# Gated cross-attention and mixture of experts: setup merged into the attention program, later loads placed behind the first placements, gelu parts in another order

## The chip, the cores and the metric

The kernel runs on one core of a Trainium2 chip. The metric is the device time of one execution in microseconds (us). Three runs of the kernel before took 1938.36, 1944.8 and 1937.91 us; the median is 1938.36. A core has TensorE (matmul, called PE in the profile, with PEld for its weight loads), VectorE (DVE), ScalarE (ACT), GpSimd (POOL) and SyncE (SP), which issues most transfers here.

## The reference

x is 16 x 512 x 512, the context 16 x 512 x 1024. First comes a gated cross-attention with 16 heads of 32, then a gated mixture of 8 experts of which each token takes two:

```
q = layernorm(x);  k, v = split(ctx_2048)
logits = (q * 32**-0.5) @ k.T + b + (-1e12) * (position >= seq_len)
x = x + tanh(g_xattn) * softmax(logits) @ v

y = layernorm(x)
route = normalise(y) @ normalise(centroids).T + y @ w_route.T
gates = softmax over the two largest of route
h = gelu(y @ w1[e] + b1[e])
x = x + tanh(g_ffn) * sum over e of gates[e] * (h @ w2[e] + b2[e])
```

Everything is float32.

## The kernel before

The program has four blocks of engine programs, one behind another. Each ends on all engines before the next begins.

The **setup** block (L305 to L400) loads the sequence lengths, b, the gates, the centroids and w_route with seven small transfers on SP. VectorE fills rows 96 to 127 of the two stacks stA and stB with ones (L344, L345), then makes the bias and mask rows for all batches (L348 to L368, stored to HBM at L316), the normalised centroids (L358, L362, the inverse square root of 13 steps at L371, L373), and constant tiles for the later tables (L375 to L381). GpSimd makes iotas, the identity and triangle tiles (L321 to L340), ScalarE two tanh values (L388, L389), TensorE the turned routing weights (L397, L398), which VectorE copies (L383).

The **attention** block is a software pipeline over 64 groups (16 batches, 4 groups of 4 heads each). Every engine runs the same list of steps, numbered from -8 (FIRST) to 70, fully unrolled, and every engine's order inside a step is written out by hand in 16 sub-steps. In step l the logits, exp and value products are those of group l; the max product (stB against stA, L823) with its row maxima (L998) is that of group l + 2; the placing of turned queries and keys in the stacks is that of group l + 3. So the first placement is in step -3, the first max product in step -2, the first logits (L811) in step 0. A placement is six SP transfers of 256 KB (L484), from SBUF to SBUF, after four small ones with the bias rows (L513). The negated maxima go to stB the same way in the step before the logits (L533).

Once a batch, x and the keys are loaded two batches ahead (L497, L498, steps with l divisible by 4), the values one batch ahead (L505), the residual at L554. VectorE takes the statistics of x (L982, L989), GpSimd makes the query scale out of them (`query_scale`, L607 to L623, called at L648) and regroups the keys (L604), ScalarE normalises x into the queries (L687), and TensorE turns queries and keys (L798); ScalarE takes the high part (L698), VectorE the low part (L974). Batch 0's and batch 1's x and keys and batch 0's values are the first five transfers of the block.

A short piece of **table** steps (L1054 to L1100) sorts the tokens by expert.

The **block loop** (L1198 to L1448) then runs over blocks of 512 tokens of one expert, in steps that each do the front of one block and the back of the block before. It is a hardware loop of 18 rounds with two steps in its body. In a step TensorE turns the gathered rows (`turn`, L1283) in two pairs, with the second product of the block before between and behind them (`second`, first half L1318, second half L1322), then the token ranks (L1293) and the first product of this block, m = 0 and m = 1, each 12 matmuls (L1332). ScalarE and VectorE split each float32 operand in a high and a low part. After the first product ScalarE does gelu (L1373) for m = 0 and 1 and then the high parts (L1376) for both; VectorE does the low parts (L1437) for both at the end of its step, behind the search for the tokens of a later block (`find_tokens`, L1434). The second product's half m waits for low part m (f_hs, L1299). VectorE also makes the low part of the expert's first weights (L1416), a 128 x 1024 subtraction. GpSimd gathers the rows of the next block with four indirect transfers (L1233), waits for the output rows of ScalarE (L1260; L1365 makes them), and adds them to the output with four more (L1263). Two tiny instructions on GpSimd, `carry_wait` (L1229), tell the other engines how far it is.

## Time and profile before

| | |
|---|---|
| Median of three runs | 1938.36 us |
| The profiled execution | 1941.25 us |
| Its span | 1939.5 us, 32926 instructions |
| TensorE busy | 1733.0 us (89%) |
| VectorE busy | 1381.7 us (71%) |
| GpSimd busy | 1249.5 us (64%) |
| ScalarE busy | 1170.1 us (60%) |
| Mean granted TensorE clock | 0.98 |

In the page's picture of 40 slices (48.5 us each) TensorE is at 0, 5 and then 9 tenths up to slice 28; slices 29 to 31 hold the tables at 6 to 9 tenths with a granted clock that falls to 5 and 7 tenths in two slices, and from there to the end it is at 9 or 8 tenths again. VectorE is at 5 tenths in the first slice, GpSimd at 2, ScalarE at 1. The chain of work that ended last is read from its end back; here it consists of GpSimd's indirect transfers (L1233 7% of the span, L1263 5%) and of issue time.

In a timeline row the first number is the start, the second the time that the merged instructions of the row cover. In brackets stands how long the engine was idle before it and what ended that. TensorE works at one of two levels, 1.2 and 2.4 GHz; the column with the granted clock says which share of the higher it was given.

### The profile page before, as it was taken

The page shows a single profiled execution, that of the slowest core. Times are in us where ns is not written, and L with a number is a line of the kernel's source. Part 1 is how long each engine was busy: PE and PEld are TensorE (multiplying, and loading weights), DVE is VectorE, ACT ScalarE, POOL GpSimd, SP SyncE. Part 2 cuts the span into 40 slices and gives each one's busy share as a digit, 9 for nine tenths or more (in the row PEclk, how much of TensorE's full clock was granted, in tenths as well). Part 3 has the DMA queues.
Part 4 walks back from the last instruction along what each step waited for, and adds up shares of the span by engine and source line. Part 5 has one row for each costly group of instructions (what it writes and reads, how often), then busy time and mean ns, then how long its engine had stood idle before and what let it go on. Part 6 is the DMA issues. An engine that isn't in the chain of part 4 may idle for free. (4 is left out here: it accounts for less than half of the span.)

```text
span 1939.5 us, 32926 instructions
## 1 busy us (share of the span) xinstructions
PE 1733.0 (89%) x9696; PEld 1039.5 (54%) x9697; DVE 1381.7 (71%) x2983; ACT 1170.1 (60%) x2044; POOL 1249.5 (64%) x1507
## 2 busy tenths in 40 slices
PE   0599999999999999999999999984699989999897
PEld 0244555555555555555555555533477767777775
DVE  5568778878878778788778787733666666665665
ACT  1066677676776776776766767663355555555554
POOL 2057577585675776675766857550577777777776
PEclk9999999999999999999999999995799999999999
DMA  3888899898898998998998979643488787868774
GB/s 111 100 175 168 129 203 160 150 208 145 159 193 160 169 183 139 191 179 132 200 154 159 198 112 188 121 133 97 89 153 148 144 142 139 154 130 148 134 146 65
DMA packets 173069, 291.46 MB, mean 150 GB/s; under 512 B 37983, under 2 KB 42079, under 8 KB 172945
## 3 DMA queue, kind: packets, MB, share of 16 engines
q1 hardware_dynamic: 140016, 222.26, 59.2%
q0 software_dynamic: 32928, 67.68, 20.0%
q8 instruction: 61, 1.00, 0.3%
q14 instruction: 64, 0.52, 0.1%
HBM read 127.09 MB, written 71.63 MB: 102 GB/s over the span
## 5 line engine op out<-in xcount | busy, mean ns | idle before, releaser
L998 DVE TENSOR_REDUCE bank<-bank 128x1 f32<-128x512 f32 x1024 | 696.2, 690 | 256.4 <-PE bank L823 248.2
L714 ACT ACTIVATE prob<-bank 128x512 f32<-128x512 f32 x1024 | 593.0, 597 | 359.1 <-PE bank L811 357.7
L659 POOL TENSOR_TENSOR prob<-prob 128x512 f32<-128x512 f32 x256 | 320.7, 1289 | 325.9 <-PE bank L771 325.9
L811 PE MATMUL bank<-stB,stA 100*128 100x512 f32 x1024 | 477.1, 467 | 19.7 <-ACT prob L714 13.6
L823 PE MATMUL bank<-stA,stB 98*128 98x512 f32 x1024 | 423.6, 416 | 31.7 <-DMA stA<-regrouped_then_w 17.5
L811 PEld LDWEIGHTS bank<-stB,stA 100*128 100x128 f32 x1024 | 193.4, 189 | 253.3 <-ACT prob L714 177.5
L663 POOL TENSOR_TENSOR prob<-prob 128x512 f32<-128x512 f32 x256 | 320.3, 1290 | 0.0
L771 PE MATMUL bank<-prob,vin 128*32 128x512 f32 x2048 | 272.7, 605 | 0.7 <-ACT prob L714 0.7
L1263 POOL DMA_INDIRECT out_dram<-yout,scatter_ids x144 | 226.4, 1572 | 52.6 <-issue 52.0
L1195 PE MATMUL bankb<-w_hi,gelu_parts 128*128 x576 | 199.1, 406 | 47.2 <-DVE gelu_parts L1437 47.2
L823 PEld LDWEIGHTS bank<-stA,stB 98*128 98x128 f32 x1024 | 197.9, 193 | 79.2 <-DVE bank L998 37.1
L1233 POOL DMA_INDIRECT rows_in<-xn_rows,gather_ids x152 | 183.6, 1208 | 85.9 <-DVE rows_in L1444 44.9
L1195 PE MATMUL bankb<-turned_parts,w_parts 128*128 128x512 f32 x888 | 218.2, 401 | 0.0
L1195 PEld LDWEIGHTS bankb<-turned_parts,w_parts 128*128 128x128 f32 x888 | 165.4, 190 | 37.6
L1195 PEld LDWEIGHTS bankb<-w_hi,gelu_parts 128*128 128x128 f32 x576 | 108.2, 188 | 78.7 <-issue 55.5
L1347 ACT ACTIVATE turned_parts<-bankb 128x512 fp32r<-128x512 f32 x148 | 82.7, 596 | 94.8 <-PE bankb L1283 83.4
L1365 ACT ACTIVATE yout<-out_with_bias,row_gates 128x512 f32<-128x512 f32 x144 | 92.4, 712 | 61.3 <-DVE out_with_bias L1428 61.3
L1437 DVE TENSOR_TENSOR gelu_parts<-gelu,gelu_parts 128x512 fp32r<-128x512 f32 x74 | 47.8, 688 | 107.0 <-ACT gelu_parts L1376 107.0
L784 PE MATMUL bank<-prob,ones 128*32 128x512 f32 x1024 | 123.1, 598 | 0.0
L1373 ACT ACTIVATE gelu<-bankb,b1s 128x512 f32<-128x512 f32 x74 | 51.0, 689 | 113.8 <-PE bankb L1195 113.8
L1195 PE MATMUL bankb<-regrouped_then_w,gelu_parts 128*128 x288 | 114.2, 397 | 0.0
L687 ACT ACTIVATE regrouped_then_w<-x_k_then_w,q_shift,rstd 128x512 f32<-128x512 f32 x64 | 83.1, 1307 | 37.3 <-POOL q_shift L623 37.3
(181 smaller groups left out, 2234.1 us busy)
## 6 DMA issues: line engine op xcount, KB each, us to landing
stB<-regrouped_then_w SPq DMA_DIRECT2D x192, 256.0 KB, 5.9
stA<-regrouped_then_w SPq DMA_DIRECT2D x192, 256.0 KB, 6.8
x_k_then_w<-in_x_dram SPq DMA_DIRECT2D x16, 1024.0 KB, 8.2
x_k_then_w<-in_ctx_dram SPq DMA_DIRECT2D x16, 1024.0 KB, 12.5
vin<-in_ctx_dram SPq DMA_DIRECT2D x16, 1024.0 KB, 9.3
xres<-in_x_dram SPq DMA_DIRECT2D x16, 1024.0 KB, 6.9
out_dram<-xres SPq DMA_DIRECT2D x16, 1024.0 KB, 7.5
xn_rows<-xn SPq DMA_DIRECT2D x64, 256.0 KB, 5.4
```

What stands on the lines that cost most here:

```text
L659: pool.tensor_tensor(first[:, j, :], first[:, j, :], more[:, j, :], ALU.add).then_inc(s_acc, 1)
L663: pool.tensor_tensor(first[:, j, :], first[:, j, :], then[:, j, :], ALU.add).then_inc(s_acc, 1)
L714: act.activation(prob_of(st, 0, u)[:, j, :], psS[j % 2][:, :], ACT.Exp).then_inc(s_exp, 1)
L771: last = pe.matmul(psO[DH * j:DH * (j + 1), :], vin[:, vpar, kt, c0:c0 + DH], p[:, j, :], start=(u == 0), stop=(u == NT - 1), skip_group_c ...
L784: last = pe.matmul(bank[DH * j:DH * (j + 1), :], ones[:, 0:DH], p[:, j, :], start=(u == 0), stop=(u > 0), skip_group_check=True, tile_posi ...
L811: pe.matmul(psS[j % 2][:, :], stA[0:100, g, j, kt * P:(kt + 1) * P], stB[0:100, g, j, :], start=True, stop=True).then_inc(s_qk, 1)
L823: pe.matmul(psM[s % 2][:, :], stB[0:98, g, j, i * P:(i + 1) * P], stA[0:98, g, j, :], start=True, stop=True).then_inc(s_m, 1)
L998: dve.tensor_reduce(mx[:, s // 4, s % 4:s % 4 + 1], psM[s % 2][:, :], AX.X, ALU.max).then_inc(s_mx, 1)
L1195: last = pe.matmul(bank, wts(p), mov(q), start=start and i == 0, stop=stop and i == 2)
L1233: pool.indirect_dma_start(rows[:, par, c, :], None, xn_d, bass.IndirectOffsetOnAxis(ap=gids[:, par, c:c + 1], axis=0), bounds_check=TOK - ...
L1263: pool.indirect_dma_start(out_rows, bass.IndirectOffsetOnAxis(ap=sids[:, h, c:c + 1], axis=0), yout[:, h, c, :], None, bounds_check=TOK - ...
L1365: act.activation(yout[:, st.h, c, :], ysum[:, c, :], ACT.Copy, scale=gate[:, st.h, c:c + 1]).then_inc(f_yo, 1)
```

## The change

It has three parts.

1. The setup's work is no longer a block of its own but stands inside the attention block. SP issues three of the small loads, then batch 0's x and keys, then the other four small loads, waits for the bias rows, stores them, and waits for both fills. The fill of stA goes from VectorE to ScalarE (four copies of a constant), that of stB to GpSimd, behind its constant tiles. VectorE does the bias steps first (`set_bias`, step -8), then the statistics of batch 0, then the query scale of batch 0 (`query_scale` takes the engine as an argument; later batches stay on GpSimd), then the centroid steps and constant tiles (`set_routes`). TensorE turns the routing weights in step -2 into another bank.
2. Batch 1's x is loaded behind the placement of step -3, batch 0's values behind that of step -2, batch 1's keys behind the maxima of step -1. VectorE's statistics of batch 1 come ten sub-steps later in steps -2 and -1.
3. In the block loop ScalarE does gelu 0, high part 0, gelu 1, high part 1. VectorE does low part 0 at the end of its step and low part 1 in the next step, behind the first two turned parts.

The diff, cut to its core (the moved instructions are otherwise the same):

```diff
+                SET_POOL = 14
+                SET_BIAS = 12
+                SET_DVE = 17 + RSQRT_STEPS
...
-                with nc.Block() as block:
-                    @block.sync
-                    def _(sp):
-                        sp.dma_start(len_i[:, :], lens.rearrange("b a -> a b").to_broadcast([P, B])).then_inc(s_load, 16)
...
-                        sp.dma_start(wro, w_route).then_inc(s_load, 16)
-                        sp.wait_ge(s_dve, 13)
-                        sp.dma_start(bm_d, b_split[:, :, :].bitcast(F32)).then_inc(s_put, 16)
-                        sp.wait_ge(s_put, 16)
-                    @block.gpsimd
...
-                    def _(pool):
-                        pool.iota(pos_i, pattern=[[1, BLK]], base=0, channel_multiplier=0).then_inc(s_pool, 1)
-                        pool.iota(pos4_i[:, :], pattern=[[P, BLK // P]], base=0, channel_multiplier=1).then_inc(s_pool, 1)
...
-                    def _(dve):
-                        dve.memset(stA[96:P, :, :, :].bitcast(F32), 1.0)
-                        dve.memset(stB[96:P, :, :, :].bitcast(F32), 1.0)
-                        dve.wait_ge(s_load, 16 * 7)
-                        dve.wait_ge(s_pool, 3)
-                        dve.tensor_copy(pos4[:, :], pos4_i[:, :]).then_inc(s_dve, 1)
-                        dve.tensor_copy(len_f[:, :], len_i[:, :]).then_inc(s_dve, 1)
...
-                    def _(act):
-                        act.wait_ge(s_load, 16 * 7)
...
@@ -461,6 +368,24 @@
                 for n in range(FIRST, G + LAST):
                     step(Step(None, n, G))
+            def query_scale(eng, st):
+                b = (st.l + 4) // 4
+                par = b % 2
+                c = lambda k: b * LN1 + k
+                eng.wait_ge(s_stat, 8 * (b + 1))
...
+                def load_batch(b):
+                    par = b % 2
+                    sp.dma_start(xin[:, par, :, :], x_d[b:b + 1].rearrange("a p i d -> p (a i) d")).then_inc(s_x[par], 16)
+                    sp.dma_start(kin[:, par, :, :], c_d[b:b + 1, :, :, 0:D].rearrange("a p i d -> p (a i) d")).then_inc(s_k[par], 16)
+                def load_v(b):
+                    sp.dma_start(vin[:, b % 2, :, :], c_d[b:b + 1, :, :, D:2 * D].rearrange("a p i d -> p (a i) d")).then_inc(s_v[b % 2], 16)
...
                     if st.g() == 0:
-                        par = (st.l // 4) % 2
-                        if st.on(8):
-                            if st.rnd is not None or st.l >= 0:
...
-                            sp.dma_start(kin[:, par, :, :], c_d[bass.ds(b, 1), :, :, 0:D].rearrange("a p i d -> p (a i) d")).then_inc(s_k[par], 16)
-                    if st.g() == 1 and st.on(4):
-                        par = (st.l // 4 + 1) % 2
-                        if st.rnd is not None or st.l >= 4:
+                        if st.on(8) and st.l >= 0:
+                            sp.wait_ge(s_xg, st.batch(1, 0, 1))
+                            sp.wait_ge(s_kg, st.batch(1, 0, 1))
+                            load_batch(st.batch(1, 8, 0))
+                        if st.l == FIRST:
+                            sp.dma_start(len_i[:, :], lens.rearrange("b a -> a b").to_broadcast([P, B])).then_inc(s_load, 16)
+                            sp.dma_start(len_c[:, 0:1], lens).then_inc(s_load, 16)
+                            sp.dma_start(b_row, b_in.rearrange("(a s) -> a s", a=1).to_broadcast([B, S])).then_inc(s_load, 16)
+                            load_batch(0)
+                            sp.dma_start(gates_in[:, 0:1], g_xattn.rearrange("(a s) -> a s", a=1).to_broadcast([P, 1])).then_inc(s_set, 16)
+                            sp.dma_start(gates_in[:, 1:2], g_ffn.rearrange("(a s) -> a s", a=1).to_broadcast([P, 1])).then_inc(s_set, 16)
+                            sp.dma_start(cen, cent).then_inc(s_set, 16)
+                            sp.dma_start(wro, w_route).then_inc(s_set, 16)
+                            sp.wait_ge(s_dve, SET_BIAS)
+                            sp.dma_start(bm_d, b_split[:, :, :].bitcast(F32)).then_inc(s_put, 16)
+                            sp.wait_ge(s_put, 16)
+                            sp.wait_ge(s_ones, 2)
+                    if st.g() == 1 and st.on(4) and st.l >= 0:
+                        if st.l >= 4:
                             sp.wait_ge(s_pv, st.batch(4 * PV, 0, 0))
-                        b = st.batch(1, 4, 0)
-                        sp.dma_start(vin[:, par, :, :], c_d[bass.ds(b, 1), :, :, D:2 * D].rearrange("a p i d -> p (a i) d")).then_inc(s_v[par], 16)
+                        load_v(st.batch(1, 4, 0))
                     if st.on(3):
                         g = st.g(3)
...
                         i, before = turn_of(st, "TK")
                         sp.wait_ge(s_took[i], before + 1)
                         place_rows(stA, 1, g, 1, turnedL)
+                    if st.l == -3:
+                        sp.dma_start(xin[:, 1, :, :], x_d[1:2].rearrange("a p i d -> p (a i) d")).then_inc(s_x[1], 16)
+                    if st.l == -2:
+                        load_v(0)
                     if st.on(1):
                         i, before = turn_of(st, "MT")
...
                         for t in range(2):
                             sp.dma_start(stB[98 + t:99 + t, st.g(1), :, :].bitcast(F32), mT[HG * t:HG * t + HG, :].bitcast(F32)).then_inc(s_md[(st.l + 1) % 2], 16)
+                    if st.l == -1:
+                        sp.dma_start(kin[:, 1, :, :], c_d[1:2, :, :, 0:D].rearrange("a p i d -> p (a i) d")).then_inc(s_k[1], 16)
                     if st.g() == 1 and st.on(-5):
...
                         if st.rnd is not None or st.l >= 8:
                             sp.wait_ge(s_x1[par], st.bpair(16, 0, 0))
                             sp.wait_ge(s_xn2, st.count(1, -4, 0))
+                        if st.l == 0:
+                            sp.wait_ge(s_dve, SET_DVE)
...
+                pool.wait_ge(s_pool, SET_POOL)
+                pool.memset(stB[96:P, :, :, :].bitcast(F32), 1.0).then_inc(s_ones, 1)
+                pool.wait_ge(s_ones, 2)
                 def step(st):
+                    if st.l == -4:
+                        pool.wait_ge(s_ln1, LN1)
+                    elif st.g() == 0 and st.on(4):
+                        query_scale(pool, st)
                     if st.g() == 0 and st.on(4):
-                        query_scale(st)
                         regroup_k(st)
...
+                act.wait_ge(s_pool, 8)
+                for g in range(NG):
+                    last = act.activation(stA[96:P, g, :, :].rearrange("p h s -> p (h s)"),
+                                          ones[96:P, 0:1].to_broadcast([P - 96, HG * S]), ACT.Copy)
+                last.then_inc(s_ones, 1)
+                act.wait_ge(s_set, 16 * 4)
+                act.activation(tanh_a[:, :], gates_in[:, 0:1], ACT.Tanh).then_inc(s_act, 1)
+                act.activation(tanh_f[:, :], gates_in[:, 1:2], ACT.Tanh).then_inc(s_act, 1)
+                act.wait_ge(s_act, 2)
                 all_steps(act, step)
...
+                def turn_routes():
+                    pe.wait_ge(s_set, 16 * 4)
+                    pe.wait_ge(s_dve, SET_DVE - 2)
+                    for k in range(KD):
+                        pe.transpose(psO[:, 2 * E * k:2 * E * k + E], cen2[:, k * P:(k + 1) * P], ident[0:E, 0:E])
+                        last = pe.transpose(psO[:, 2 * E * k + E:2 * E * k + 2 * E], wro[:, k * P:(k + 1) * P],
+                                            ident[0:E, 0:E])
+                    last.then_inc(s_pe, 1)
                 def step(st):
+                    if st.l == -2:
+                        turn_routes()
                     for s in range(16):
                         u, j = s // 4, s % 4
...
                             kt, g = NT - 1 - u, st.g()
+                            if st.l == 0 and s == 0:
...
                             last.then_inc(done, 1)
...
+                def set_bias():
+                    dve.wait_ge(s_load, 16 * 3)
+                    dve.wait_ge(s_pool, 3)
+                    dve.tensor_copy(len_cf[:, 0:1], len_c[:, 0:1]).then_inc(s_dve, 1)
+                    dve.tensor_copy(pos[:, :], pos_i).then_inc(s_dve, 1)
+                    dve.tensor_copy(len_f[:, :], len_i[:, :]).then_inc(s_dve, 1)
...
+                    dve.wait_ge(s_dve, 9)
+                    dve.tensor_tensor(b_split[:, 1, :], b_all, b_split[:, 0, :].bitcast(F32),
+                                      ALU.subtract).then_inc(s_dve, 1)
+                    dve.tensor_copy(pos4[:, :], pos4_i[:, :]).then_inc(s_dve, 1)
+                    dve.tensor_copy(qcol[:, :], qcol_i[:, :]).then_inc(s_dve, 1)
...
+                def set_routes():
+                    dve.wait_ge(s_set, 16 * 4)
+                    dve.tensor_tensor_reduce(cen2, cen, cen, 1.0, 0.0, ALU.mult, ALU.add,
+                                             cn[:, 0:1]).then_inc(s_dve, 1)
+                    dve.wait_ge(s_dve, SET_BIAS + 1)
+                    dve.tensor_scalar(cn[:, 1:2], cn[:, 0:1], NORM_EPS * NORM_EPS, None, ALU.max).then_inc(s_dve, 1)
...
+                    rsqrt(dve, cn[:, 0:1], cn[:, 2:3], cn[:, 1:2], s_dve, lambda k: SET_BIAS + 2 + k)
+                    dve.wait_ge(s_dve, SET_BIAS + 2 + RSQRT_STEPS)
+                    dve.tensor_scalar(cen2, cen, cn[:, 0:1], None, ALU.mult).then_inc(s_dve, 1)
+                    dve.memset(ranks[0:TILES, :, :], float(P)).then_inc(s_dve, 1)
...
+                def take_routes():
+                    dve.wait_ge(s_pe, 1)
+                    dve.tensor_copy(routeT[:, :, :], psO[:, 0:KD * 2 * E].rearrange("p (k e) -> p k e", k=KD)).then_inc(s_dve, 1)
                 def step(st):
+                    if st.l == FIRST:
+                        set_bias()
+                    if st.l == -4:
+                        query_scale(dve, st)
+                        set_routes()
+                    if st.l == -2:
+                        take_routes()
                     for s in range(16):
...
                             route(st, s)
-                        if st.g() in (2, 3) and s in (0, 3) and st.on(8 - st.g()):
-                            stats(st, 2 * (st.g() - 2) + s // 3)
-                        if st.g() in (2, 3) and s in (2, 4) and st.on(8 - st.g()):
-                            aggregate(st, 2 * (st.g() - 2) + s // 4)
+                        late = 10 if st.l in (-2, -1) else 0
+                        if st.g() in (2, 3) and s - late in (0, 3) and st.on(8 - st.g()):
+                            stats(st, 2 * (st.g() - 2) + (s - late) // 3)
+                        if st.g() in (2, 3) and s - late in (2, 4) and st.on(8 - st.g()):
+                            aggregate(st, 2 * (st.g() - 2) + (s - late) // 4)
...
@@ -1371,7 +1412,6 @@
                                 act.wait_ge(f_hs, st.front(KE, -1, m + 1))
                             act.activation(gelu[:, m, :], psH[m][:, :], ACT.Gelu, bias=b1s[:, st.par(), m:m + 1]).then_inc(f_g, 1)
-                        for m in range(KE):
                             act.wait_ge(f_g, st.front(KE, 0, m + 1))
                             act.activation(hT[:, 0, m, :], gelu[:, m, :], ACT.Copy).then_inc(f_hhi, 1)
@@ -1385,6 +1425,11 @@
                     def take_turned(st, k):
                         dve.wait_ge(f_xhi, st.front(KD, 0, k + 1))
                         dve.tensor_tensor(xTb[:, 1, k, :], bank_of(st, USE[k])[:, :], xTb[:, 0, k, :].bitcast(F32), ALU.subtract).then_inc(f_use, 1)
+                    def gelu_lo(st, off, m):
+                        dve.wait_ge(f_hhi, st.front(KE, off, m + 1))
+                        dve.tensor_tensor(hT[:, 1, m, :], gelu[:, m, :], hT[:, 0, m, :].bitcast(F32), ALU.subtract).then_inc(f_hs, 1)
                     def mark_tiles(blk, expert):
@@ -1412,6 +1457,8 @@
                         mark_tiles(st.block(2), expert_ahead)
                         take_turned(st, 0)
                         take_turned(st, 1)
+                        if not st.first:
+                            gelu_lo(st, -1, 1)
                         dve.wait_ge(f_whi, st.front(1, 0, 1))
                         dve.tensor_tensor(w1p[:, 1, :, :], weights_of(w1_all, expert), w1p[:, 0, :, :].bitcast(F32), ALU.subtract).then_inc(f_wlo, 1)
                         take_turned(st, 2)
@@ -1432,9 +1479,7 @@
                         dve.tensor_copy(sids[:, st.par(), :], gids[:, st.par(), :]).then_inc(f_sid, 1)
                         dve.wait_ge(f_sid, st.steps(1, 0, 1))
                         find_tokens(bank_of(st, USE[KD]), st.block(2), st.par(), lambda per, k: st.steps(per, 2, k))
-                        for m in range(KE):
-                            dve.wait_ge(f_hhi, st.front(KE, 0, m + 1))
-                            dve.tensor_tensor(hT[:, 1, m, :], gelu[:, m, :], hT[:, 0, m, :].bitcast(F32), ALU.subtract).then_inc(f_hs, 1)
+                        gelu_lo(st, 0, 0)
```

## Rows read from the trace of the kernel before

**Rows 1.** Timeline from the start, setup: start us, us, engine, line, operation [idle before <- releaser].
```profile
5.51 0.20 ACT L388 ACTIVATE tanh_a<-xT 128x1 f32<-128x1 f32 x1 [3.45 <-DMA xres<-in_L_ffn_w_route_dram]
...
11.10 6.88 DVE L345 MEMSET stB<- 32x8192 f32 x1 [1.66 <-issue]
...
18.00 0.17 DVE L348 CAST positions_by_chunk<-xT 128x4 f32<-128x4 int32 x1
...
22.35 0.32 SPq L316 DMA_DIRECT2D bias_mask_rows<-xres  x1
...
22.43 0.14 DVE L121 TENSOR_SCALAR xT<-xT 8x1 int32<-8x1 int32 x1
...
24.77 0.47 DVE L373 TENSOR_SCALAR xres<-xres,xT 8x512 f32<-8x512 f32 x1
...
29.29 0.41 SPq L497 DMA_DIRECT2D x_k_then_w<-in_x_dram  x1
...
34.83 0.69 DVE L982 BATCH_NORM_STATS2 regrouped_then_w<-x_k_then_w 128x6 f32<-128x512 f32 x1 [5.82 <-DMA x_k_then_w<-in_x_dram]
```

**Rows 2.** Timeline of the attention program's start.
```profile
38.21 0.26 POOL L616 TENSOR_SCALAR varx<-mv 128x4 f32<-128x4 f32 x1 [34.55 <-DVE mv L989]
...
43.11 4.44 ACT L687 ACTIVATE regrouped_then_w<-x_k_then_w,q_shift,rstd 128x512 f32<-128x512 f32 x4 [37.30 <-POOL q_shift L623]
...
49.38 2.01 SPq L484 DMA_DIRECT2D stB<-regrouped_then_w  x3
...
64.22 0.77 PE L823 MATMUL bank<-stA,stB 98*128 98x512 f32 x1 [14.65 <-DMA stA<-regrouped_then_w]
...
98.41 0.79 PE L811 MATMUL bank<-stB,stA 100*128 100x512 f32 x1 [3.50 <-DMA stB<-regrouped_then_w]
```

**Rows 3.** Waits, 1385 to 1940 us: us in total, times, longest us.
```profile
POOL hold L1229 <- ACT yout L1365: 47.7, 34, 11.2
...
PE bankb L1195 <- DVE gelu_parts L1437: 47.2, 36, 1.4
```

**Rows 4.** Timeline of GpSimd alone in the block loop.
```profile
1704.69 1.55 POOL L1263 DMA_INDIRECT out_dram<-yout,scatter_ids  x1 [0.30 <-issue]
...
1717.58 1.54 POOL L1263 DMA_INDIRECT out_dram<-yout,scatter_ids  x1 [0.30 <-issue]
...
1722.85 1.98 POOL L1233 DMA_INDIRECT rows_in<-xn_rows,gather_ids  x1 [0.31 <-issue]
...
1725.13 1.00 POOL L1233 DMA_INDIRECT rows_in<-xn_rows,gather_ids  x1 [0.30 <-DMA out_dram<-yout,scatter_ids]
...
1734.92 1.54 POOL L1263 DMA_INDIRECT out_dram<-yout,scatter_ids  x1 [0.31 <-issue]
...
1749.70 1.55 POOL L1263 DMA_INDIRECT out_dram<-yout,scatter_ids  x1 [0.30 <-issue]
```
**Rows 5.** Timeline of one step of the block loop.
```profile
1714.07 0.69 ACT L1373 ACTIVATE gelu<-bankb,b1s 128x512 f32<-128x512 f32 x1 [1.10 <-PE bankb L1195]
...
1716.87 0.69 ACT L1373 ACTIVATE gelu<-bankb,b1s 128x512 f32<-128x512 f32 x1 [2.12 <-PE bankb L1195]
...
1717.46 1.14 ACT L1376 ACTIVATE gelu_parts<-gelu 128x512 fp32r<-128x512 f32 x2
...
1718.11 1.29 DVE L1437 TENSOR_TENSOR gelu_parts<-gelu,gelu_parts 128x512 fp32r<-128x512 f32 x2 [2.88 <-ACT gelu_parts L1376]
...
1719.04 0.50 PE L1195 MATMUL bankb<-w_hi,gelu_parts 128*128 x1 [1.33 <-DVE gelu_parts L1437]
...
1722.70 1.21 DVE L1416 TENSOR_TENSOR w_parts<-x_k_then_w,w_parts 128x1024 fp32r<-128x1024 f32 x1
```

**Rows 6.** Busy time by stretch; last three columns: granted clock, DMA share, GB/s.
```profile
30.00:40.00 10.00, 0.00 (x0) 0.00 (x0) 3.15 (x8) 0.00 (x0) 1.30 (x7) 1.00 0.93 329
...
90.00:100.00 10.00, 5.91 (x12) 3.02 (x12) 5.39 (x11) 0.60 (x1) 1.32 (x7) 1.00 1.07 180
```

137 lines of the change are left out of this document (50 added, 87 removed).

## The prediction

> **What bounds the kernel now.** I read the chain that ended last first. It lies wholly on GpSimd's indirect DMAs in the block loop and says nothing of the first 1300 us, so I then read the timeline from the start, and the waits and the timeline of single block steps. The span has three parts. Up to the first logit matmul at 98.41 us TensorE does almost nothing; from there to about 1300 us it is busy without a break; from about 1386 us the block loop runs 36 steps with a period of 15.1 us. The change touches the first part and the third. The middle starts earlier or later with the first part and keeps its length, because TensorE bounds it and nothing of it is edited.
>
> In the first part the reader is to see a sequence with hardly any overlap. Two VectorE fills of 6.88 us (the second begins at 11.10) stand ahead of every setup step, so the steps begin at 18.00 us and the first load is issued at 29.29, though all small loads were there by 5.51 [rows 1]. Then x arrives (34.83), VectorE takes the statistics, GpSimd makes the query scale (38.21 to 43.11), ScalarE normalises, and the first placement goes out at 49.38 [rows 1, 2]. From 49.38 the DMA engines set the pace: the max product starts only at 64.22 when the rows are placed, and the first logits, two placements later, at 98.41 [rows 2].
>
> In the block loop two bounds lie close together. TensorE waits 47.2 us in total, 36 times, for the low gelu part of VectorE; GpSimd waits 47.7 us, 34 times, for the output rows of ScalarE, 11.2 us of it once at the start, so 1.1 us in each of the others [rows 3]. Two steps take 1734.92 - 1704.69 = 30.23 us, 15.11 each [rows 4]. Without its wait TensorE would need 15.11 - 47.2/36 = 13.80; GpSimd without its wait 15.11 - 1.1 = 14.0. So the reorder can gain 1.3 us a step at most, and 1.1 if GpSimd stays as it is.
>
> **Part 1, the setup inside the attention program.** The x load goes from being SP's first DMA of a second block (29.29) to its fourth. Three small loads stand ahead of it; at 0.4 to 0.5 us for one issue (the x load takes 0.41 [rows 1]) it goes out near 2.2. Its landing took 34.83 - 29.29 = 5.54 us [rows 1], so x is there at 7.7. The bias steps on VectorE now come before the statistics: 22.35 - 18.00 = 4.35 us with the centroid reduction of about 0.7, which moves out, so 3.7 to 4.0 [rows 1]. They start when three small loads have landed, at about 4 and surely by 5.51 [rows 1], and end at 8.0 to 9.5. So the statistics start near 8.0 instead of 34.83: 26.8 us earlier. The first query scale moves from GpSimd (43.11 - 38.21 = 4.90 for 17 small steps [rows 2]) to VectorE, where 13 such steps on a narrower tile took 24.77 - 22.43 = 2.34, 0.18 each [rows 1]; 17 at 0.2 are 3.5, a further 1.4. ScalarE's normalising then starts 28.2 us earlier, at 14.9.
>
> What could be late instead: the two fills. The one of stA is now four ScalarE copies of 2048 elements. A 512-element copy takes 0.57 (1.14 for two [rows 5]), so at most 4 x 4 x 0.57 = 9.1 us from 2.4 on, 11.5. The tanh pair then waits for small loads that stand behind 2 MB, near 11, and ends by 13.5: hidden before 14.9, 1.4 us to spare. The fill of stB on GpSimd has no row of its own; VectorE takes 6.88 for the shape [rows 1], which gives 3.7 to 10.6, and twice that ends at 17.5. SP needs both only before the first bias rows, and those must be out by 21.2 (49.38 - 28.2). The centroid steps and rank fills (at most 29.29 - 22.35 = 6.9 us and the 0.7 of the reduction [rows 1]) come after the query scale, end near 22, and can hold the first low part back by 0.8, behind two placements that are queued anyway. I cost these at nothing; without that cover each is worth 1 to 3 us.
>
> **Part 2, the second batch's loads behind the placements.** Before, five loads of 1 MB moved at 329 GB/s while nothing else wanted the DMA engines [rows 6], 3.2 us each. Now x of batch 1, v of batch 0 and k of batch 1 are queued behind placements 0, 1 and 2. Between the landing of a placement and the issue of the next lie some 2.4 us, so the first two cost 3.2 - 2.4 = 0.8 each. The third meets DMA engines whose share is 1.07 from 90 to 100 us [rows 6], where batch 2's x and k follow, so I charge it in full, 3. Sum 4.6, bounds 0 and 9.6. SP is also held behind them only for their issue, 0.5 each. The late statistics of batch 1 (steps -2 and -1, moved by ten sub-steps of about 0.8) find x landed, and GpSimd's scale is wanted only at the key regroup of step 0.
>
> Part 1 and 2 give 28.2 - 4.6 = 23.6. Here a row speaks against the plan: gathers on GpSimd that take 1.00 us take 1.98 when VectorE runs its 1024-wide subtraction with both inputs in SBUF (1722.70 to 1723.91; the gather ends 0.9 us after it) [rows 4, 5]. The two engines do block one another. If the long GpSimd fill (3.7 to 10.6) holds VectorE's casts the same way, the bias steps start at 10.6 rather than 4 to 5.5 and x is no longer the last to come: 5 to 6 us lost. I cannot tell from before, where VectorE was inside a fill while GpSimd worked. The Trainium skill ("SBUF — State Buffer", Who interferes with whom) calls the shared port pair an exclusive lock that is held for a whole instruction, with casts and tensor_scalar among the operations that want it; by it VectorE would stand still until the fill ends. I take 23.6 for the start, since GpSimd is the one that is held in the rows shown, and keep 18 as rival (e); bounds 15 and 28.
>
> **Part 3, gelu order.** In the traced step the products of m=0 are done at 1714.07, of m=1 at 1716.87, and ScalarE then does gelu 1, copy 0, copy 1, so that VectorE starts low part 0 at 1718.11 and TensorE its second product at 1719.04 after 1.3 us of idling [rows 5]. Afterwards copy 0 follows gelu 0 at 1714.7; VectorE comes to low part 0 when the token search is done, near 1715.3, and ends it at 1716.0, before TensorE asks for it (its turns end near 1717.7). The wait is gone. Low part 1 goes into the next step behind two turned parts; it is ready some 1 us before TensorE reaches the second half. No table load shows between gelu and copy [rows 5], so alternating them costs nothing. Late next are TensorE itself (13.8) and GpSimd (14.0). GpSimd's 14.0 holds the stretching of gathers, 1.0 us in the step shown. The subtraction that causes it now starts about 1.6 us earlier against TensorE's own work, while GpSimd falls back to be the later one, so part of the overlap should slide off the gathers onto the scatters; and scatters beside a two-input subtraction show no stretch (1.54 at 1717.58, beside 1718.11) [rows 4, 5]. I take 13.9 a step: 1.2 x 36 = 43, rounded to 42 for the first and last steps. Bounds: 54 (also the turns' waits for VectorE gone, an estimated 13.6) and 12 (each step as in rival a).
>
> **Sum.** 23.6 + 42 = 65.6 us. The profiled run took 1941.25 with a span of 1939.5, so its like would take 1875.7; the median of the runs, 1938.4, is 2.9 lower: 1938.4 - 65.6 = 1872.8.
>
> **Rivals.**
> (a) GpSimd's gathers eat the loop's gain. The step from 1734.92 to 1749.70 took 14.78 [rows 4] without a wait for output rows, so GpSimd alone filled it. If every step becomes like it, the gain is (15.11 - 14.78) x 36 = 12, total 36, 1903; half way to the forecast it is 1888. For it: GpSimd already bounds such a step. Against: the waits are there in 34 of 36 steps [rows 3], so it is rare.
> (b) Both parts run at their floors: start 28, loop 54 at 13.6 us a step: 1856.
> (c) Slower: the lock between VectorE and GpSimd takes hold of every indirect DMA of the loop. The two low parts (0.65 each), the subtraction (1.21) and the tile marks (0.55) add up to 3.1 us a step; all of it on top of about 13.5 (14.0 less half of the 1.0 us stretch shown) is 16.6, 1.5 us longer than now, 54 us in the loop; less the start's 23.6 gives 1969. It decides from a period of 15.1 + 23.6/36 = 15.8 on. Against it: the scatter beside low part 0 is not stretched [rows 4, 5].
> (d) The start does not move as it says: a fill or the tanh pair holds ScalarE past 14.9 or SP past 21, and placements queue behind all three loads; an estimated gain of 10 (28.2 less 9.6 for three loads in full and some 9 for a fill that ends late). With the loop as forecast 1886.
> (e) The long GpSimd fill holds VectorE: start 18, total 60, 1878. For it: GpSimd is held by VectorE in [rows 4, 5], and the lock would act both ways. Against: no row shows VectorE held.
>
> **How the numbers follow.** Forecast 1873, chance 0.37; (e) 0.25; (a) 0.17, (b) 0.09, (c) 0.04, (d) 0.08. The range of 8 in 10 takes in (e), (d), the milder half of (a) and most of the way to (b), which leaves out about 0.17: 1858 to 1900. About 0.5%, 9.7 us, is what a measurement of this kernel can tell from no change: only (c) ends above it; the 0.02 is for loops that stop between (a) and (c). Faster 0.94, same 0.02, slower 0.04.
>
> **What would show it.** The first statistics near 8 us (near 14 if the fill blocks VectorE), ScalarE's normalising near 15 to 20, the first max product near 36 to 42, the first logits near 73 to 80, and the attention's length from there unchanged. In the loop: TensorE's wait for the low gelu part near zero, GpSimd's wait for ScalarE's output rows gone or small, period 13.6 to 14.2, gathers of 1.0 to 1.1 us. I am wrong if the gathers grow, if the period stays above 14.5, or if step 0 of the attention waits for k of batch 1.

## The result, and the profile after

The changed kernel takes 1895.47 us (median of 4, 1892.71 to 1897.25) against 1939.86 us for the kernel before, measured beside it: a ratio of 0.9766, 95% interval 0.9742 to 0.979. The forecast was 1872.8 us, range 1858 to 1900. The sign and the range held; the gain is 44 us where 65.6 were summed.

The span fell from 1939.5 to 1895.5 us, by 44.0. To find where, I compare the two traces at marks that both have: the load of the residual x in the first and second batch, and the first gather of the block loop. First the kernel before, then the changed one (start us, us, engine, line, operation).

```profile
183.63 0.45 SPq L554 DMA_DIRECT2D xres<-in_x_dram  x1
...
1359.04 3.48 POOL L1233 DMA_INDIRECT rows_in<-xn_rows,gather_ids  x1 [44.88 <-DVE rows_in L1444]
```
```profile
166.56 0.44 SPq L506 DMA_DIRECT2D xres<-in_x_dram  x1
...
1341.34 3.47 POOL L1274 DMA_INDIRECT rows_in<-xn_rows,gather_ids  x1 [44.21 <-DVE rows_in L1489]
```

The first part brings 17.1 us by the second batch and 17.7 by the first gather of the block loop. The remaining 26.3 us come from the loop.

**The start.** Timeline of the changed kernel's first steps:

```profile
2.18 0.42 SPq L410 DMA_DIRECT2D x_k_then_w<-in_x_dram  x1
2.38 7.30 ACT L711 ACTIVATE stA<-ones 32x2048 fp32r<-32x2048 f32 x4 [0.32 <-POOL ones L587]
...
3.73 6.92 POOL L601 MEMSET stB<- 32x8192 f32 x1
...
3.99 6.95 DVE L982 CAST positions<-prob 128x512 f32<-128x512 int32 x1
...
11.23 0.20 ACT L715 ACTIVATE tanh_a<-xT 128x1 f32<-128x1 f32 x1 [1.55 <-DMA xres<-in_L_ffn_w_route_dram]
...
14.12 0.67 DVE L968 BATCH_NORM_STATS2 regrouped_then_w<-x_k_then_w 128x6 f32<-128x512 f32 x1
...
20.81 4.45 ACT L649 ACTIVATE regrouped_then_w<-x_k_then_w,q_shift,rstd 128x512 f32<-128x512 f32 x4 [9.29 <-DVE q_shift L387]
...
42.22 0.77 PE L808 MATMUL bank<-stA,stB 98*128 98x512 f32 x1 [13.76 <-DMA stA<-regrouped_then_w]
...
76.98 0.77 PE L796 MATMUL bank<-stB,stA 100*128 100x512 f32 x1 [3.29 <-DMA stB<-regrouped_then_w]
```

The reader is to see VectorE's second cast begin at 3.99, inside the GpSimd fill of 3.73 to 10.65, and end 0.3 us behind it. Everything on VectorE moves by that. ScalarE's normalising starts 22.3 us earlier than before (43.11 in [rows 2]), the first max product 22.0 and the first logits 21.4 earlier ([rows 2]). So the two loads that now stand behind placements 0 and 1 cost 0.9 us together (22.3 less 21.4).

Between the first logits and the second batch the lead falls from 21.4 to 17.1. The place is the second step of the attention. Rows of the changed kernel's timeline around it: the negated maxima (L1087) once in each step, SP's queue, and TensorE's wait.

```profile
68.33 0.44 SPq L482 DMA_DIRECT2D x_k_then_w<-in_ctx_dram  x1
68.88 0.51 SPq L410 DMA_DIRECT2D x_k_then_w<-in_x_dram  x1
69.43 0.51 SPq L411 DMA_DIRECT2D x_k_then_w<-in_ctx_dram  x1
...
86.23 1.33 SPq L480 DMA_DIRECT2D stB<-regrouped_then_w  x2
87.66 0.41 SPq L506 DMA_DIRECT2D xres<-in_x_dram  x1
88.12 0.58 SPq L415 DMA_DIRECT2D vin<-in_ctx_dram  x1
...
94.83 0.18 DVE L1087 TENSOR_SCALAR regrouped_then_w<-bank 128x16 fp32r<-128x16 f32 x1
...
97.42 0.80 PE L796 MATMUL bank<-stB,stA 100*128 100x512 f32 x1 [3.36 <-DMA stB<-regrouped_then_w]
...
118.98 0.17 DVE L1087 TENSOR_SCALAR regrouped_then_w<-bank 128x16 fp32r<-128x16 f32 x1
```

That step takes 118.98 - 94.83 = 24.15 us. The one of before took 19.3 (its negated maxima at 116.27 and 135.55), so 4.9 are lost there; at the second batch's mark the loss is 4.3. Three loads of 1 MB are issued from 68.33 on and two more from 87.66 on. The placements of 256 KB between them land 8.3 to 12.0 us after their issue; the median over the whole run is 5.8 (stB) and 6.8 us (stA). The maxima of 86.23 stand behind these placements in SP's queue. The stretches of the same moment (columns: PE, weight load, VectorE, ScalarE, GpSimd busy us; the last three are granted clock, DMA share, GB/s):

```profile
94.00:96.00 2.00, 0.06 (x1) 0.00 (x0) 1.12 (x4) 1.38 (x2) 2.00 (x2) 0.97 1.06 152
96.00:98.00 2.00, 0.58 (x1) 0.50 (x2) 0.00 (x0) 0.00 (x0) 0.25 (x1) 0.50 1.05 318
98.00:100.00 2.00, 2.00 (x8) 1.41 (x6) 0.70 (x1) 1.01 (x2) 0.00 (x0) 0.50 1.04 386
100.00:102.00 2.00, 2.00 (x9) 0.20 (x8) 1.29 (x2) 0.67 (x2) 0.00 (x0) 0.50 0.98 339
102.00:104.00 2.00, 2.00 (x18) 0.85 (x18) 0.70 (x1) 1.07 (x2) 0.00 (x0) 0.82 1.09 141
```

TensorE waits 3.36 us, and its clock stands at the lower level (0.50, 1.2 GHz) from 96 to 102 us: a logits matmul (L796) takes 0.80 us at 97.42 and 0.50 at 104.91. The wait and the low clock together are the loss. How much each takes is seen from gelu_only, a run reported below whose start is that of the kernel before, unedited. There the second step took 21.2 us instead of 19.3. TensorE waited 1.25 us in it against 0.88, and its granted clock was 0.67 and 0.50 from 116 to 120 us against 1.00. The longer wait is 0.4 of these 1.9 us, which leaves some 1.5 for the low clock. So almost 2 of the 4.9 us can come without the change. In the runs below that keep the changed start the step takes 22.4 to 24.1 us.

**The block loop.** Groups of GpSimd's instructions from 1390 to 1870 us of the changed kernel (count | busy us, mean ns | idle before):

```profile
L1304 POOL DMA_INDIRECT out_dram<-yout,scatter_ids x134 | 224.9, 1678 | 40.8 <-issue 38.1 <-DVE gather_ids L1452 2.7
L1274 POOL DMA_INDIRECT rows_in<-xn_rows,gather_ids x135 | 143.9, 1066 | 36.2 <-issue 33.3 <-POOL hold L1270 2.6 <-DMA out_dram<-yout,scatter_ids 0.3
L1270 POOL TENSOR_TENSOR hold<-ones 128x1 f32<-128x1 f32 x67 | 51.6, 770 | 3.1 <-issue 1.2 <-ACT yout L1406 1.1
```

TensorE's 47.2 us of waiting for the low gelu part and GpSimd's 47.7 us for the output rows ([rows 3]) are gone; of the second 1.1 are left. GpSimd now hardly waits for another engine; nearly all of its idle time is issue time. The same group of before had scatters of 1573 ns, gathers of 1196 and holds of 501: the gathers got shorter, the scatters and holds longer.

For the comparisons below I averaged GpSimd's timeline over 34 steps of each kernel (us a step; 'hold' is the instruction `carry_wait` of L1270, 'wait' is GpSimd's wait for the output rows ahead of it). The steps are those of one profiled execution, the times are medians of four:

| kernel | step | 4 gathers | 4 scatters | 2 holds | wait | time us, ratio |
|---|---|---|---|---|---|---|
| before | 15.09 | 4.77 | 6.29 | 1.02 | 1.04 | 1939.9 |
| changed | 14.34 | 4.26 | 6.72 | 1.55 | 0.03 | 1895.5, 0.9766 |
| gelu_only | 14.28 | 4.21 | 6.80 | 1.36 | 0.13 | 1911.3, 0.9847 |
| start_only | 14.99 | 4.61 | 6.35 | 1.03 | 1.06 | 1920.7, 0.9902 |
| fill_act | 14.14 | 4.14 | 6.79 | 1.30 | 0.12 | 1884.9, 0.9726 |
| loads_moved | 14.12 | 4.14 | 6.79 | 1.31 | 0.09 | 1890.0, 0.9748 |
| w_low_in_four | 14.27 | 4.15 | 6.72 | 1.15 | 0.30 | 1897.6, 0.9775 |
| lows_apart | 14.34 | 4.23 | 6.84 | 1.24 | 0.24 | 1891.9, 0.9736 |
| w_low_from_bank | 14.93 | 4.14 | 6.75 | 0.99 | 1.20 | 1922.3, 0.9903 |
| fill_shared_loads_spread | 14.34 | 4.19 | 6.74 | 1.49 | 0.11 | 1881.9, 0.9685 |
| gelu_in_bank | 14.09 | 4.22 | 6.34 | 1.23 | 0.50 | 1887.6, 0.9714 |
| gpsimd_more | 14.39 | 4.15 | 6.95 | 1.20 | 0.01 | 1897.6, 0.9770 |
| tensor_more | 14.38 | 4.44 | 6.61 | 1.37 | 0.15 | 1897.4, 0.9765 |
| both_mended | 14.10 | 4.25 | 6.33 | 1.52 | 0.14 | 1874.8, 0.9656 |

Ratios are against the kernel before on the same chip; their intervals reach 0.0016 to 0.0027 to either side. The profiled execution lay up to 4.7 us from its median (w_low_in_four, below it). Executions of one and the same kernel differ by up to 9.9 us (fill_act, 1882.88 to 1892.77), so 0.2 us a step (7 us in the whole) between two rows of the table does not by itself show an effect.

**When an instruction of GpSimd is stretched.** I sorted every gather and scatter from 1390 to 1870 us by whether, at its start, a VectorE subtraction with both inputs in SBUF (gelu low part, weight low part) was running. In the changed kernel 32 scatters start inside one: mean 1.91 us. 36 scatters have one that begins only after they have started: 1.56 us. 5 gathers start inside one, 1.91 us, the others take 1.03. In the kernel before no scatter starts inside one and 27 gathers do (1.56 us in the mean); there 4 gathers are also held that had started 0.18 to 0.47 us ahead of the subtraction (2.30 and 2.64 us). One case of the changed kernel:

```profile
1725.35 0.69 DVE L1432 TENSOR_TENSOR gelu_parts<-gelu,gelu_parts 128x512 fp32r<-128x512 f32 x1
1725.51 1.97 POOL L1304 DMA_INDIRECT out_dram<-yout,scatter_ids  x1 [0.30 <-issue]
...
1727.79 1.55 POOL L1304 DMA_INDIRECT out_dram<-yout,scatter_ids  x1 [0.30 <-issue]
```

The subtraction ends at 1726.04, the scatter at 1727.48: 1.44 us later, about what an unhindered one takes. In 31 of the 32 the rest after the subtraction's end is 1.43 to 1.47 us. So the instruction waits for the subtraction's end and then runs whole. The hold is caught too, but with a difference that is easily missed. Here it starts 0.24 us before the first of two subtractions that follow each other:

```profile
1658.22 2.10 POOL L1270 TENSOR_TENSOR hold<-ones 128x1 f32<-128x1 f32 x1
1658.46 0.68 DVE L1432 TENSOR_TENSOR gelu_parts<-gelu,gelu_parts 128x512 fp32r<-128x512 f32 x1
1659.06 1.22 DVE L1463 TENSOR_TENSOR w_parts<-x_k_then_w,w_parts 128x1024 fp32r<-128x1024 f32 x1
1660.47 1.09 POOL L1274 DMA_INDIRECT rows_in<-xn_rows,gather_ids  x1 [0.15 <-POOL hold L1270]
```

It ends at 1660.32, with the second of the two (1660.28). With no such subtraction beside it this hold mostly takes 0.77 to 0.81 us. In all the runs of the table it ends 0.03 to 0.06 us after a subtraction (of one or, as here, of the next) whenever it started up to 0.59 us before it, and it takes 0.77 to 0.79 us whenever it started 0.62 us or more before. So a later moment inside the instruction counts, not the start of its row. For the scatters of the changed kernel that moment comes early: they were free with a start 0.17 us ahead.

### The profile page after: what moved, and what is told of

Read it like the earlier page. It is cut to its first block and busy times, and to the rows that moved or that the text cites. A ratio compares the mean times of both kernels' runs of the same rounds, so it can differ in the third digit from the quotient of the medians.

```text
span 1895.5 us, 32938 instructions
## 1 busy us (share of the span) xinstructions
PE 1733.6 (91%) x9696; PEld 1041.0 (55%) x9697; DVE 1382.8 (73%) x2997; ACT 1185.8 (63%) x2048; POOL 1269.8 (67%) x1491
## 5 line engine op out<-in xcount | busy, mean ns | idle before, releaser
L796 PE MATMUL bank<-stB,stA 100*128 100x512 f32 x1024 | 477.8, 467 | 22.0 <-ACT prob L676 13.6
L796 PEld LDWEIGHTS bank<-stB,stA 100*128 100x128 f32 x1024 | 193.7, 190 | 256.0 <-ACT prob L676 176.5
L1304 POOL DMA_INDIRECT out_dram<-yout,scatter_ids x144 | 241.5, 1677 | 44.0 <-issue 41.3
L1274 POOL DMA_INDIRECT rows_in<-xn_rows,gather_ids x152 | 166.2, 1094 | 85.2 <-DVE rows_in L1489 44.2
L1427 DVE TENSOR_TENSOR turned_parts<-bankb,turned_parts 128x512 fp32r<-128x512 f32 x148 | 95.3, 685 | 47.6 <-ACT turned_parts L1388 40.5
L1236 PEld LDWEIGHTS bankb<-w_hi,gelu_parts 128*128 128x128 f32 x576 | 108.3, 188 | 39.0 <-issue 15.7
L1324 PE MATMUL bankb<-ident,rows_in 128*128 128x128 f32 x592 | 80.7, 279 | 31.9 <-DMA rows_in<-xn_rows,gather_ids 31.0
```

The costliest lines, as they stand in the source:

```text
L796: pe.matmul(psS[j % 2][:, :], stA[0:100, g, j, kt * P:(kt + 1) * P], stB[0:100, g, j, :], start=True, stop=True).then_inc(s_qk, 1)
L1236: last = pe.matmul(bank, wts(p), mov(q), start=start and i == 0, stop=stop and i == 2)
L1274: pool.indirect_dma_start(rows[:, par, c, :], None, xn_d, bass.IndirectOffsetOnAxis(ap=gids[:, par, c:c + 1], axis=0), bounds_check=TOK - ...
L1304: pool.indirect_dma_start(out_rows, bass.IndirectOffsetOnAxis(ap=sids[:, h, c:c + 1], axis=0), yout[:, h, c, :], None, bounds_check=TOK - ...
L1427: dve.tensor_tensor(xTb[:, 1, k, :], bank_of(st, USE[k])[:, :], xTb[:, 0, k, :].bitcast(F32), ALU.subtract).then_inc(f_use, 1)
```

## The experiments

**gelu_only and start_only: the two halves apart.** The first is the kernel before with the order of the gelu parts alone:

```diff
                             act.activation(gelu[:, m, :], psH[m][:, :], ACT.Gelu, ...)
-                        for m in range(KE):
                             act.wait_ge(f_g, st.front(KE, 0, m + 1))
                             act.activation(hT[:, 0, m, :], gelu[:, m, :], ACT.Copy)
...
                         take_turned(st, 1)
+                        if not st.first:
+                            gelu_lo(st, -1, 1)
...
-                        for m in range(KE):
-                            dve.wait_ge(f_hhi, st.front(KE, 0, m + 1))
-                            dve.tensor_tensor(hT[:, 1, m, :], gelu[:, m, :], hT[:, 0, m, :]...)
+                        gelu_lo(st, 0, 0)
```

The second is the changed kernel with these lines as they were.

> The kernel before with the new order of the gelu parts alone. Theory A (the two halves of the change add up, and the trace of after splits their gain): the block loop's step falls from 15.09 us to 14.34 us over 36 steps, which is 27 us, and nothing else moves: ratio 0.986, about 1912.5 us. Rival B (the order of the gelu parts brings the 42 us that were forecast for it, and the start's gain was lost somewhere on the way): 1897 us, ratio 0.978. Rival C (the order brings the loop little by itself, and the start's shift did the rest): over 1925 us.

> The changed kernel with the old order of the gelu parts: the new start alone. Theory A: the loop's step stays at 15.1 us as before, the first logits stand 21.4 us earlier, 4.3 to 4.8 us of that are given back in the second step of the attention, and the end comes 17 us earlier: ratio 0.991, about 1922 us. Rival B (the start's 23.6 us are lost further on by more than the records show): over 1930 us. Rival C (nothing is given back): 1916 us.

Measured: 0.9847 (0.9831 to 0.9864) and 0.9902 (0.9886 to 0.9919). The profiled spans are 28.1 and 24.8 us below that of before; the steps are 14.28 and 14.99 us. The medians give 28.0 and 18.6 us, 46.6 together against 44.4 for the whole change beside its own runs of before, so within the intervals the halves add up. The single profiles do not say it as clearly (52.9 against 44.0): that of start_only is 4.2 us below its median. In start_only the second step of the attention takes 23.96 us too (negated maxima at 95.25 and 119.21), so that loss does not come from the loop's edit. Theory A held for both, but for its "nothing else moves": in gelu_only the second step took 21.2 us, as said above.

**fill_act: the long GpSimd fill taken away.**

```diff
-                pool.memset(stB[96:P, :, :, :].bitcast(F32), 1.0).then_inc(s_ones, 1)
...
-                for g in range(NG):
-                    last = act.activation(stA[96:P, g, :, :]...)
-                last.then_inc(s_ones, 1)
+                for stack in (stA, stB):
+                    for g in range(NG):
+                        last = act.activation(stack[96:P, g, :, :]...)
+                    last.then_inc(s_ones, 1)
```

> The changed kernel with the one long GpSimd fill (6.92 us, of the constant rows of the second stack) taken off GpSimd and put on ScalarE behind its other four fills. ScalarE's fills then end near 16.5 us, and its first normalisation starts only at 20.8 us in the changed kernel. Theory A (VectorE's first cast of 6.95 us is held by the GpSimd fill): the cast takes under 1 us, the bias steps end some 6 us earlier, the x statistics start when x has landed, about 4 to 5 us earlier than 14.12 us, and the end comes 4 to 5 us earlier than the changed kernel: about 1890.5 us, ratio to the kernel before 0.974. Rival B (the cast was long because it waits for a load or for its own first use, and not for GpSimd): the cast stays near 7 us and the time near 1895 us. Rival C (the start is then held by ScalarE's eight fills, or the four microseconds are given back in the load queue further on): the cast is short and the time is still 1894 to 1896 us.

Measured: 1884.93 us, 0.9726 (0.9699 to 0.9753). Timeline of this kernel:

```profile
4.00 0.40 DVE L982 CAST positions<-prob 128x512 f32<-128x512 int32 x1
...
7.67 0.70 DVE L968 BATCH_NORM_STATS2 regrouped_then_w<-x_k_then_w 128x6 f32<-128x512 f32 x1
...
17.22 4.44 ACT L648 ACTIVATE regrouped_then_w<-x_k_then_w,q_shift,rstd 128x512 f32<-128x512 f32 x4
...
38.44 0.77 PE L808 MATMUL bank<-stA,stB 98*128 98x512 f32 x1 [13.79 <-DMA stA<-regrouped_then_w]
```

The cast takes 0.40 instead of 6.95 us and the statistics start 6.45 us earlier. This is theory A: the fill had held VectorE. ScalarE's eight fills take the place of it as what is late (VectorE's scale is ready near 14.3, normalising starts at 17.22), so the first max product gains 3.8. The first gather of the loop is 3.4 us earlier than in the changed kernel; most of the rest of the span's 11.9 us (some 7) is a loop step of 14.14 instead of 14.34, with no edit in the loop. That part was not foreseen; it is taken up below.

**loads_moved: batch 1's k a step earlier, batch 2's x and k behind the placement of the maxima.**

> The changed kernel with two things moved in the queue of loads: the second batch's k load goes one step earlier (behind the first v load), and the third batch's x and k loads go behind the placement of the row maxima of their step rather than ahead of it. Theory A (TensorE's wait of 3.36 us and the low clock of 0.50 that follows it, in the second step, come from the placement of the maxima that queues behind 3 MB of loads): the second step's 24.15 us fall to about 19.5 us and the end comes 4 to 4.5 us earlier: about 1891 us. Rival B (the bytes only move, and hold the placements of the step before or the statistics of the next batch instead): within 1 us of the changed kernel, 1895 us. Rival C (the k load ahead of the first maxima delays the first logits by 3 us and the loop keeps that): 1898 us.

Measured: 1889.99 us, 0.9748 (0.973 to 0.9766). The time looks like theory A, but the trace says rival B. Negated maxima and TensorE's wait in this kernel:

```profile
95.67 0.17 DVE L1091 TENSOR_SCALAR regrouped_then_w<-bank 128x16 fp32r<-128x16 f32 x1
...
114.72 0.17 DVE L1091 TENSOR_SCALAR regrouped_then_w<-bank 128x16 fp32r<-128x16 f32 x1
...
118.22 0.79 PE L800 MATMUL bank<-stB,stA 100*128 100x512 f32 x1 [4.56 <-DMA stB<-regrouped_then_w]
...
140.01 0.17 DVE L1091 TENSOR_SCALAR regrouped_then_w<-bank 128x16 fp32r<-128x16 f32 x1
```

The second step is cured (19.05 us), the third, 18.43 in the changed kernel, now takes 25.29 with a wait of 4.56, and the first gather of the loop stands at 1343.02, 1.7 later than in the changed kernel. What the whole run gained is again the loop, at 14.12 a step.

**fill_shared_loads_spread: both faults of the start mended.** The fill of stB is half ScalarE's, half GpSimd's and there only behind VectorE's bias steps; and of the 1 MB loads one goes out in a step where two or three stood together.

```diff
+                pool.wait_ge(s_dve, SET_BIAS)
+                pool.memset(stB[96:P, 2:4, :, :].bitcast(F32), 1.0).then_inc(s_ones, 1)
...
-                    if st.l == -1:
+                    if st.l == -2:
                         sp.dma_start(kin[:, 1, :, :], c_d[1:2, :, :, 0:D]...)
+                    if st.l == -1:
+                        sp.wait_ge(s_xg, 1)
+                        sp.dma_start(xin[:, 0, :, :], x_d[2:3]...)
+                    if st.l == 1:
+                        sp.wait_ge(s_kg, 1)
+                        sp.dma_start(kin[:, 0, :, :], c_d[2:3, :, :, 0:D]...)
+                    if st.l == 2:
+                        load_v(1)
```

> The changed kernel with two things moved in its first steps. First the fill of the second stack's constant rows: half on ScalarE behind its own four, half on GpSimd, only once VectorE's bias steps are done. Second the loads of 1 MB, one a step where two or three stood together: the second k load goes a step earlier, the third x load behind the maxima of step -1, the third k load behind those of step 1, the second v load into step 2. Theory A: the first cast takes 0.4 us, the normalisation starts near 14.5 us rather than 20.81 us, the first product of maxima near 35.5 to 36 us rather than 42.22 us; and no step of the first four is longer than 20.5 us, since no placement of the maxima queues behind more than 2 MB. Together 6 plus 4.5 us: about 1885 us, with the loop's step as in the changed kernel. Rival B (VectorE's statistics are held by the late fill as the cast was): the start is earlier by 3 us only. Rival C (the wait moves to another step, as it did when two of the loads were moved): a step of 24 to 25 us is found again and the 4.5 us don't come.

Measured: 1881.93 us, 0.9685 (0.9669 to 0.9701). Timeline of this kernel:

```profile
7.70 0.69 DVE L976 BATCH_NORM_STATS2 regrouped_then_w<-x_k_then_w 128x6 f32<-128x512 f32 x1
7.78 3.51 POOL L608 MEMSET stB<- 32x4096 f32 x1 [4.11 <-DVE qcol L1007]
...
8.53 0.66 DVE L976 BATCH_NORM_STATS2 regrouped_then_w<-x_k_then_w 128x6 f32<-128x512 f32 x1
...
14.50 4.45 ACT L656 ACTIVATE regrouped_then_w<-x_k_then_w,q_shift,rstd 128x512 f32<-128x512 f32 x4 [0.90 <-DVE q_shift L387]
...
35.96 0.76 PE L816 MATMUL bank<-stA,stB 98*128 98x512 f32 x1 [13.79 <-DMA stA<-regrouped_then_w]
...
89.24 0.17 DVE L1095 TENSOR_SCALAR regrouped_then_w<-bank 128x16 fp32r<-128x16 f32 x1
...
108.65 0.17 DVE L1095 TENSOR_SCALAR regrouped_then_w<-bank 128x16 fp32r<-128x16 f32 x1
```

Statistics run beside a GpSimd fill at 0.66 us, unhindered, so rival B falls. No step of 24 us is found, so rival C falls too, though the first takes 20.7 where 20.5 was the bound. Normalising starts at 14.50 (the forecast's 14.9). The steps that took 20.1 and 24.15 us take 20.7 and 19.4, the granted clock stays at 1.00 from 84 to 114 us, and the first gather of the loop comes at 1331.20, 10.1 us before that of the changed kernel: theory A. Its loop step is 14.34, the same as that of the changed kernel, so the two profiles differ by the start alone.

**w_low_in_four, lows_apart, w_low_from_bank: what holds GpSimd in the loop.** The weight low part as four quarters; the gelu low part one instruction earlier; the weight low part replaced by two instructions of the same length that read PSUM (the true low part of w1 is left out there).

```diff
-                        dve.tensor_tensor(w1p[:, 1, :, :], weights_of(w1_all, expert), w1p[:, 0, :, :]..., ALU.subtract)
+                        dve.wait_ge(f_xhi, st.front(KD, 0, 3))
+                        for half in range(2):
+                            low = dve.tensor_tensor(w1p[:, 1, 2 * half:2 * half + 2, :]...,
+                                                    bank_of(st, USE[2])[:, :], xTb[:, 0, 2, :].bitcast(F32), ALU.subtract)
```

> The changed kernel with VectorE's weight low part (1.22 us a step, both inputs in SBUF) written as four instructions of a quarter each. The block loop's step was 14.12 to 14.34 us in the four profiles that have the new gelu order, and its GpSimd is never idle beyond 0.1 us a step. Theory A (GpSimd is held by each such VectorE instruction to its end, and can slip in between two instructions): hold falls from 1.3 to 1.55 us a step to about 0.8, the step to 13.9 us, the time to about 1885 us. Rival B (instructions that follow each other without a gap hold GpSimd as one): hold stays at 1.3 us or more and the step at 14.1 to 14.4 us, 1890 to 1897 us. Rival C (GpSimd isn't held by this instruction at all): nothing changes in hold either.

> The changed kernel with the gelu low part of the block before placed between VectorE's first and second turned low part, so that it no longer stands directly ahead of the 1.22 us weight low part: an instruction that reads PSUM (0.68 us) lies between the two. Theory A (it is the run of 0.69 and 1.22 us together that holds GpSimd): hold falls by up to 0.5 us a step, the step to about 13.9 us, about 1885 us. Rival B (GpSimd waits for the last of them wherever the first stands): hold stays at 1.3 to 1.5 us, 1890 to 1897 us. Rival C (the second turned part is late by 0.6 us and TensorE's turns with it): the step rises to 14.6 us, 1905 us.

> The changed kernel with the weight low part replaced by two VectorE instructions of 0.68 us that read one input from PSUM (the third turned bank) and write the same place: VectorE's work is as long (1.36 against 1.22 us) and the two-SBUF-input form is gone. The output then lacks the true low part of w1. Theory A (GpSimd is the loop's bound, at some 13.6 us of its own instructions and issue, and the rest of its step is time in which the two-SBUF-input instructions hold it): hold falls to under 0.6 us a step, scatters to under 6.6, the step to 13.6 to 13.8 us, the time to 1872 to 1880 us. Rival B (TensorE and the landing of the gathered rows bound the step, and GpSimd's held time is slack): the step stays within 14.1 to 14.4 us. Rival C (any VectorE instruction holds GpSimd): hold stays over 1.2 us.

Measured: 0.9775 (0.9759 to 0.9792), 0.9736 (0.9719 to 0.9752) and 0.9903 (0.9883 to 0.9922). In four pieces the holds fall to 1.15 us a step, and GpSimd does get in between two pieces: 15 gathers start inside one of the first three pieces and end 0.96 to 0.97 us after that piece, though the next follows at once. But the subtraction now takes 1.42 instead of 1.22 us on VectorE and a wait for the output rows of 0.30 comes up; the time is no better, and the holds stay above theory A's 0.8. With the low parts apart the holds fall to 1.24 and the step stays: rival B by the time. With the weight low part out of SBUF, holds fall to 0.99, the 0.97 that stand where nothing interferes (0.77 and 0.20). GpSimd's step less its wait is then 13.73 us against 14.31 in the changed kernel, so the weight low part costs GpSimd 0.6 a step. But the step rose to 14.93: the replacement has to wait for the third turned bank and frees the banks later, and TensorE's turns and the output rows came late (ScalarE's wait for the turns 56.2 us against 35.7 from 1390 to 1880 us, GpSimd's for the rows 1.20 a step). Rival C falls, and theory A's holds under 0.6 and step of 13.8 were not met either. My edit was not neutral on the other chain, so it gives the price of the holding and no answer on what bounds the loop.

**gelu_in_bank: the gelu low parts read PSUM.**

```diff
-  act.activation(gelu[:, m, :], psH[m][:, :], ACT.Gelu, ...)
+  act.activation(psH[m][:, :], psH[m][:, :], ACT.Gelu, ...)
-  act.activation(hT[:, 0, m, :], gelu[:, m, :], ACT.Copy)
+  act.activation(hT[:, 0, m, :], psH[m][:, :], ACT.Copy)
-  dve.tensor_tensor(hT[:, 1, m, :], gelu[:, m, :], hT[:, 0, m, :]...)
+  dve.tensor_tensor(hT[:, 1, m, :], psH[m][:, :], hT[:, 0, m, :]...)
...
-                                pe.wait_ge(f_g, st.front(KE, -1, m + 1))
+                                pe.wait_ge(f_hs, st.front(KE, -1, m + 1))
```

> The changed kernel with the gelu written back into its PSUM bank rather than to SBUF, so that both gelu low parts (2 x 0.69 us a step) read one input from PSUM and only the weight low part (1.22 us) is left with both inputs in SBUF. TensorE's next first product into a bank waits for the low part instead of the gelu. In the changed kernel GpSimd's own time (step less its wait for yout) is 14.31 us, its four scatters take 6.72 us against 6.38 where nothing lies beside them, its two holds 1.55 against 0.97. Theory A (each two-SBUF-input instruction holds GpSimd): scatters fall to about 6.4 us, holds to 1.2 or less, GpSimd's own time to 13.7 to 13.9 us; the step falls with it as far as the other chain (gathered rows, turns, second product, yout) lets it, to 13.9 to 14.1 us: 1880 to 1887 us. Rival B (the other chain bounds the step already at 14.1 to 14.3 us): the own time falls, a wait for yout of 0.3 us or more comes in, and the time stays at 1890 to 1896 us. Rival C (the holding is not by form): scatters and holds stay as long.

Measured: 1887.56 us (1887.24 to 1888.58), 0.9714 (0.9698 to 0.973). The scatters' group in this kernel, 1390 to 1870 us:

```profile
L1304 POOL DMA_INDIRECT out_dram<-yout,scatter_ids x136 | 215.7, 1586 | 43.2 <-issue 38.9 <-DVE gather_ids L1452 4.3
```

A scatter that starts inside the new subtraction:

```profile
1662.07 0.69 DVE L1432 TENSOR_TENSOR gelu_parts<-bankb,gelu_parts 128x512 fp32r<-128x512 f32 x1 [0.20 <-ACT gelu_parts L1416]
1662.38 1.58 POOL L1304 DMA_INDIRECT out_dram<-yout,scatter_ids  x1 [0.30 <-issue]
```

The subtractions take 0.69 us as before and 34 scatters start inside one, at 1.57 us in the mean, where the 32 of the changed kernel took 1.91. Over all scatters it is 1586 ns instead of 1678, 6.34 us a step. The form of the instruction is the cause, not VectorE being busy. GpSimd's step less its wait fell by 0.7 us, to 13.59. Of these 0.4 are the scatters; the 0.3 of the holds come and go without an edit (1.30 in fill_act). A wait of 0.50 came in and the step fell only to 14.09, and the time is 0.6 us above theory A's range, with half of rival B in it. Since fill_act and loads_moved have 14.14 and 14.12 with the loop unedited, the cure of the scatters is shown, a gain of the step by it is not.

**gpsimd_more and tensor_more: a known cost on either side.** Three more one-column additions on GpSimd a step, and the rank product made twice.

> The changed kernel with three more one-column additions on GpSimd in each step of the block loop, behind its gathers (the second hold, of the same form, takes 0.20 us there, so about 0.4 to 0.6 us a step together). Theory A (GpSimd bounds the step): the step grows by all of it, from 14.3 to 14.7 to 14.9 us, 36 times: 1910 to 1917 us. Rival B (another chain bounds it): the step grows by under 0.2 us, below 1902 us.

> The changed kernel with the rank product of each block made twice on TensorE (0.40 us more a step) ahead of the first products. Theory A (GpSimd bounds the step, TensorE has slack): under 0.15 us a step, at most 1901 us. Rival B (TensorE's chain bounds it, or both chains are joined in one ring: gathers, turns, second product, yout, scatters, gathers): the step grows by 0.3 to 0.4 us, 1906 to 1910 us.

Measured: 0.977 (0.9754 to 0.9787) and 0.9765 (0.9741 to 0.979), both as the changed kernel, steps of 14.39 and 14.38. The additions took 0.49 us a step:

```profile
1649.40 0.49 POOL L1297 TENSOR_TENSOR hold<-ones 128x1 f32<-128x1 f32 x3
1649.83 0.19 POOL L1270 TENSOR_TENSOR hold<-ones 128x1 f32<-128x1 f32 x1
```

and the step grew by 0.05. Theory A missed: GpSimd's own sum of instructions is not a fixed bound. With the additions its holds fell from 1.55 to 1.20 and the idle time ahead of the first scatter from 0.30 to 0.21. On TensorE the second rank product took less than I had said: the eight matmuls last 0.62 us against 0.40 for four, and what follows starts 0.22 us later, not 0.40. The step grew by 0.04, which fits slack on TensorE, but 0.22 us is no more than the same loop code varies by, so this run does not decide against rival B.

**both_mended: the mended start and the gelu in its bank together.**

> The changed kernel with what was found at its two ends put together: the fill shared and late and the 1 MB loads spread over the steps (start and second step), and the gelu written back into its bank (both gelu low parts read PSUM). Theory A (the two add up): the block loop's first gather at 1331 to 1332 us, as with the start's edits alone, scatters at 6.34 us and the step at 14.1 us as with the bank alone: 10 us plus 8 us less than the changed kernel, 1874 to 1878 us, ratio 0.966. Rival B (the loop's step of 14.1 to 14.35 us is set by how the steps fall against each other and not by the low parts): 1882 us as with the start's edits alone.

Measured: 1874.8 us (1873.89 to 1875.69), 0.9656 (0.964 to 0.9672). First gather at 1330.85 us, step 14.10, scatters 6.33: the numbers are those of theory A. The start's 10 us and the shorter scatters are the edits'. The step is not shown to be: 14.10 was also reached, within 0.04, with the loop unedited, and GpSimd's step less its wait is 13.96 here against 14.02 in fill_act. It is faster than both kernels, 20 us under the changed one (0.9656 against 0.9766).

## Why the prediction was right or wrong, point by point

- **x first, bias steps from 4 us.** Right to the first instruction (x issued at 2.18, first cast 3.92). The statistics came at 14.12, not 8.0, by rival (e). With the fill gone they start at 7.67. The chain of the forecast was right but for the fill, which I had costed at nothing. It cost 28.2 - 22.3 = 5.9 us, as (e) said (5 to 6). The failed step is the choice "I take 23.6 for the start, since GpSimd is the one that is held in the rows shown". Those rows showed only a VectorE instruction that began first. The Trainium skill ("SBUF — State Buffer", Who interferes with whom) says of the port pair that VectorE and GpSimd share that whoever issues first has it for the whole instruction. Here the fill began at 3.73 and the cast at 3.99, so the cast's 6.95 us agree.
- **ScalarE's fill and the tanh pair.** 7.30 us (bound 9.1), tanh at 11.23 (near 11): right, and hidden.
- **Three loads behind the placements, 4.6.** The first two 0.9 together (1.6 charged), the third with its neighbours 4.3 (3 charged): 5.2 in sum. The size was near, the mechanism only half: not the placement behind the load but the placement of the maxima one step later waits, and the lower clock behind that wait is part of the price. loads_moved shows that the wait goes where the loads go; fill_shared_loads_spread that it vanishes when no two stand together.
- **The middle keeps its length.** Right apart from that one step: 17.1 us at the second batch, 17.0 at the last maxima, 17.7 at the first gather. The last 0.6 is not shown to be an effect of the change: the lead moves by -1.0 to +2.3 us over the tables in the other runs, whose edits do not touch them.
- **TensorE's wait for the low gelu part vanishes.** Right; no row of it is left.
- **13.9 us a step, 42 us.** Measured 14.34 and 26.3 us. This is the term that was mis-sized by most: 15.7 of the 21.6 us that the sum lacks (the start's 6.5 less the 0.6 of the tables are the rest). The failed step is "scatters beside a two-input subtraction show no stretch (1.54 at 1717.58, beside 1718.11)". That scatter had started 0.53 us before the subtraction and so was not held; in before no scatter started inside one. When the holding slid off the gathers (4.77 to 4.26), as forecast, it fell on scatters (6.29 to 6.72) and holds (1.02 to 1.55), and cost there 0.96 where it freed 0.51. GpSimd's step less its wait went from 14.05 up to 14.31, where I had it at 13.9.
- **Rivals.** (e) happened. (a) did in kind, not by the gathers but by what stands behind them, and to a smaller part than 14.78 a step. Of (c) the mechanism is real, but it takes 0.4 us of the scatters and 0.5 of the holds, and gives 0.5 back at the gathers. (d) did not happen.

**What stays open.** The same loop code ran at 14.12 to 14.34 us a step in five profiles whose only differences lie ahead of it, and half a microsecond more of GpSimd's work did not lengthen it. That fits a ring in which a later GpSimd starts its instructions at other points of VectorE's subtractions and is held less, but no run isolates it. Since each kernel has one profile and its executions differ by up to 9.9 us, the spread may lie as much between two executions of one kernel as between the edits. Gains of a few us in the whole time that come with an edit outside the loop (some 7 of the 11.9 us of fill_act's span, 0.2 us in each of 36 steps) are of this kind and are not shown to be an effect of the edit. So what bounds the loop's step at 14.1 to 14.3 us, and whether 13.9 can be had, stays open. In w_low_from_bank and gelu_in_bank GpSimd's step less its wait came down to 13.73 and 13.59, and then it waited for the output rows.

## What to carry to other kernels

Before an instruction of VectorE is moved, look at which instructions of GpSimd would start inside it in the new order; one row in which nothing was stretched proves nothing unless it started second, and a short instruction like the hold can be caught even when it started first. A fill on an idle GpSimd is not free if VectorE has a cast to do at that time; split it, give part to ScalarE, and start GpSimd's part late. Compare an edit with the spread between executions of one kernel before it is called a gain. Spread first loads by at most one large one a step and look at what small, urgent transfer is queued behind them, not only at what is queued next.

## What the runs showed of the hardware

- A GpSimd fill of 6.92 us held a VectorE cast of 128x512 (0.40 us alone) for 6.95 us. A fill of 3.51 us did not hold statistics with one input (0.66 us each). In the changed kernel a GpSimd copy from 20.86 to 25.00 us held an 8x1 multiplication of VectorE with both inputs in SBUF for 3.14 us (0.15 alone):

```profile
20.86 4.14 POOL L556 COPY regrouped_then_w<-x_k_then_w 128x2048 f32<-128x2048 f32 x1 [10.20 <-DVE q_shift L387]
...
21.70 3.14 DVE L123 TENSOR_TENSOR xT<-xT 8x1 f32<-8x1 f32 x1
```

- A scatter that starts inside a VectorE subtraction with both inputs in SBUF ends 1.43 to 1.47 us after the subtraction's end, in 31 of 32 cases; one that started 0.17 us or more before takes 1.56 us. With one input of the subtraction in PSUM it is not held (1.57 us, 34 cases). A one-column addition on GpSimd (the hold, 0.77 us alone) is still held when it started up to 0.59 us before such a subtraction, and free from 0.62 us on.
- Four instructions of a quarter each let GpSimd in between (15 gathers in w_low_in_four), at 1.42 us instead of 1.22 on VectorE.
- After 3.36 us of waiting TensorE ran at 1.2 GHz until about 102 us, though it was busy without a break from 97.42 us on. In gelu_only it fell to that level at a wait of 1.25 us; in the kernel before it did not at one of 0.88 us.
- The column with the granted clock is not enough by itself: in the kernel before it says 1.00 at 98.41 us, after a wait of 3.50 us, but the same logits matmul takes 0.79 us there and 0.50 at 108.13.
